# Narrow matrix products widened to all 128 rows in a two-layer decoder

## The reference

```python
x = x + _L0_attn_ref(_layernorm(x), t_k, t_v, t_q, W1, b1, W2, b2)        # scan over the 16 sequences
x = x + _L0_xattn_ref(_layernorm(x), ctx, mask_bf1, Wq, Wk, Wv, Wo, bo, g1, b1, g2, b2)
x = x + _L0_ffn_ref(_layernorm(x), ...)                                    # top 2 of 8 experts
x = x + _L1_attn_ref(_layernorm(x), Wq, Wk, Wv, Wo, bo)                     # ALiBi, 16 heads
x = x + _L1_xattn_ref(_layernorm(x), ctx, ctx, mask_ik0, ...)
x = x + _L1_ffn_ref(_layernorm(x), ...)                                    # top 2 of 8 experts
```

## Time and profile before

| what | value |
|---|---|
| time, median of 3 runs | 746.4 us (741.73 to 748.1) |
| profiled execution, its own time | 753.57 us |
| its span, and mean granted clock | 751.5 us, 0.848 |
| PE busy, share of the span | 603.6 us, 80% |
| DVE, ACT, POOL busy | 483.9, 431.8, 359.0 us |
| rounds of the first rotation | 16, of 6.3 to 14.1 us |
| rounds of the last attention, where steady | 5.24 us |

### The profile page before, as it was taken

One profiled execution on the slowest core, in us unless ns is written; L12 is line 12 of the kernel. 1 busy time (PEld: TensorE's weight loads), 2 busy tenths in 40 slices (PEclk: granted clock), 3 DMA queues, 4 the chain that ended last, 5 costly groups with the idle time before them and its releaser, 6 DMA issues.

```text
span 751.5 us, 18475 instructions
## 1 busy us (share of the span) xinstructions
PE 603.6 (80%) x6145; PEld 484.0 (64%) x6160; DVE 483.9 (64%) x1361; ACT 431.8 (57%) x897; POOL 359.0 (48%) x644
## 2 busy tenths in 40 slices
PE   2797999999999850999937999996997972499970
PEld 1485677777777640999924767664675651499970
DVE  7553545677767543555536999986898976255545
ACT  1452355778667311788814676765686751487840
POOL 5711332445467756466652433421445757365650
PEclk9996555989779565899968999999899996699995
DMA  7749950000000001222163000000000001222215
GB/s 193 231 168 321 330 196 1 2 2 3 1 15 16 22 22 46 72 73 71 52 216 160 2 2 3 1 3 1 2 3 8 28 19 47 53 72 69 68 37 167
DMA packets 41853, 52.59 MB, mean 70 GB/s; under 512 B 11056, under 2 KB 36897, under 8 KB 41473
## 3 DMA queue, kind: packets, MB, share of 16 engines
q1 hardware_dynamic: 37217, 42.07, 18.3%
q0 software_dynamic: 4544, 9.35, 3.8%
HBM read 40.97 MB, written 28.22 MB: 92 GB/s over the span
## 4 chain that ended last, share of the span: by engine, by line
issue 70%; PE 11%; POOL 6%; SPq 2%; DVE 2%; DMA 2%; POOLq 0%; DVEq 0%
PE p_s L1669 5%; POOL yo L1575 5%; PE p_o L1679 3%; PE p_in L1679 2%; DVE x L1626 2%; POOL to_row L1570 1%; SPq L1709 1%; PE p_pT L1661 1%; SPq L286 1%; DMA yo<-context,to_row 1%; DMA context<-xs 0%; DMA back<-yo 0%; SPq L1694 0%; SPq L1698 0%; POOLq L1569 0%
## 5 line engine op out<-in xcount | busy, mean ns | idle before, releaser
L1575 POOL DMA_INDIRECT yo<-context,to_row x78 | 76.1, 976 | 68.0 <-DVE context L1609 36.3
L1633 ACT ACTIVATE context<-pack 128x1156 f32 x78 | 90.6, 1166 | 30.8 <-DVE context L1609 13.4
L1669 PE MATMUL p_s<-xT_f,context 128*128 128x128 f32 x624 | 85.7, 282 | 0.0
L1669 PEld LDWEIGHTS p_s<-xT_f,context 128*128 128x128 f32 x624 | 79.2, 199 | 0.0
L1118 POOL DMA_INDIRECT xs<-send,x_index x64 | 64.1, 1001 | 23.9 <-issue 16.4
L1602 DVE TENSOR_SCALAR context<-p_s,context 128x128 f32<-128x128 f32 x156 | 47.5, 346 | 28.7 <-PE p_s L1669 23.8
L1312 ACT ACTIVATE x_pT<-p_pT 128x512 f32<-128x512 f32 (+1 forms) x96 | 48.8, 526 | 29.6 <-PE p_pT L1415 27.5
L1415 PE MATMUL p_pT<-sq,x_prob 128*128 128x128 f32 x320 | 59.7, 317 | 2.3 <-ACT x_pT L1312 1.6
L1640 ACT ACTIVATE context<-p_s,context 128x128 f32<-128x128 f32 x156 | 47.5, 356 | 21.4 <-PE p_s L1669 12.3
L1154 DVE TENSOR_REDUCE x_top<-p_s 128x12 f32<-128x924 f32 (+2 forms) x48 | 47.0, 1006 | 12.1 <-PE p_s L1401 12.0
L1164 DVE TENSOR_TENSOR x_prob<-p_s,x_top 128x768 f32<-128x768 f32 (+2 forms) x96 | 50.1, 577 | 0.1
(11 more groups left out here) (252 smaller groups left out, 1523.2 us busy)
## 6 DMA issues: line engine op xcount, KB each, us to landing
xs<-in_blank SPq DMA_DIRECT2D x2, 8707.5 KB, 43.3
pack<-in_pack SPq DMA_DIRECT2D x16, 578.0 KB, 8.5
context<-xs SPq DMA_DIRECT2D x78, 64.5 KB
back<-yo SPq DMA_DIRECT2D x16, 256.0 KB, 4.6
yo<-context,to_row POOLq DMA_INDIRECT x78
x<-in_x SPq DMA_DIRECT2D x4, 256.0 KB, 4.5
xs<-send,x_index POOLq DMA_INDIRECT x64
out<-x SPq DMA_DIRECT2D x4, 256.0 KB, 2.3
```

The costliest lines, as they stand in the source:

```text
L1575: nc.gpsimd.indirect_dma_start(yo[:, :], bass.IndirectOffsetOnAxis(to_row[:, n % NY, :], 0), y[:, n % NY, :], None).then_inc(y_stored[n % ...
L1633: nc.scalar.activation(ws[:, n % NW, :], pack[:, bass.ds(e, 1), :].rearrange("p a w -> p (a w)"), ACT.Copy).then_inc(ws_ready, 1)
L1669: ins = mm(p_h[n % 2][k // 2][:, P * (k % 2):P * (k % 2 + 1)], ws[:, n % NW, P * k:P * (k + 1)], xT[:, n % 2, :], start=True, stop=True)
```

## The change

Products that contracted over 1, 3 or 33 rows contract over all 128, and the rows that are added hold zeros in one of the operands:

- the bias products L854 and L1455: the weights were one row of ones and the moving operand the row of the bias; now the weights are the first column of the identity, broadcast along the columns (a one in row 0, zeros below), and the bias is row 0 of a tile of 128 rows with zeros below;
- L865 and L903: the hidden tiles `hT` and `hqT` and the weights `scan_w2T` become 128 rows high, rows 33 to 127 being zeros; POOL clears the two hidden tiles at the start, and the weights come with their zeros from one table in memory, `top_rows`;
- the masks L1389: the mask lies once, in rows 0 (or 0 to 2) of its tile, of which the rest was already cleared; the product takes all 128 rows of it, against a column that is one in these rows and zero elsewhere (the first column of the identity, or column 3 of the triangle `before`). Four transfers place the masks where 16 did.

The order of PE's products is as before. The lines of the changed kernel are from 1 to 5 higher.

```diff
-SCAN_LOADS = 6
+SCAN_LOADS = 5
+        m["first_row"] = m["eye"][:, 0:1].to_broadcast([P, P])
-        m["scan_w2T"] = sb("scan_w2T", [HID + 1, P])
+        m["scan_w2T"] = sb("scan_w2T", [P, P])
-        m["scan_b1r"] = sb("scan_b1r", [1, HID])
+        m["scan_b1r"] = sb("scan_b1r", [P, HID])
@@ start of the rotation on POOL
                 pool.wait_ge(m["loaded_rest"], 16 * m["n_rest"])
-                pool.wait_ge(m["masks_placed"], 64 * NG)
+                for n in ("hT", "hqT"):
+                    nc.gpsimd.memset(m["scan_work"][n], 0.0).then_inc(m["scan_sems"]["set_up"], 1)
+                pool.wait_ge(m["scan_sems"]["set_up"], 2)
+                pool.wait_ge(m["masks_placed"], 64)
@@ loads on SP
-                        load(w2T[0:HID, :], t["scan_w2T"], ls)
-                        load(w2T[HID:HID + 1, :], t["rows"][ROWS.index("s_b2"):ROWS.index("s_b2") + 1, :], ls)
+                        load(w2T[:, :], t["top_rows"][:, P:2 * P], ls)
-                        load(b1r[:, :], t["scan_b1"].rearrange("(a p) -> a p", a=1), ls)
+                        load(b1r[:, :], t["top_rows"][:, 2 * P:], ls)
@@ placing the masks on SP
-                        for g in range(NG):
-                            r0 = STRIP * g
-                            sp.dma_start(m["mask_0"][r0:r0 + 1, :, :].rearrange("a b k -> a (b k)"), mk_0[:, :]).then_inc(m["masks_placed"], 16)
-                            for r in range(3):
-                                sp.dma_start(m["mask_1"][r0 + r:r0 + r + 1, :, :].rearrange("a b k -> a (b k)"),
-                                             mk_1[:, r, :]).then_inc(m["masks_placed"], 16)
+                        sp.dma_start(m["mask_0"][0:1, :, :].rearrange("a b k -> a (b k)"), mk_0[:, :]).then_inc(m["masks_placed"], 16)
+                        for r in range(3):
+                            sp.dma_start(m["mask_1"][r:r + 1, :, :].rearrange("a b k -> a (b k)"), mk_1[:, r, :]).then_inc(m["masks_placed"], 16)
@@ scan, tiles and L854
-        ("hT", [HID + 1, P]), ("hqT", [HID + 1, P]), ...
+        ("hT", [P, P]), ("hqT", [P, P]), ...
-            mm(p_a, ones[0:1, :], b1r[:, :], start=False, stop=True).then_inc(a_ready, 1)
+            mm(p_a, m["first_row"], b1r[:, :], start=False, stop=True).then_inc(a_ready, 1)
@@ attention, masks L1389 and bias L1455
+        rows_on = (m["ident_bf"][:, 0:1] if mask_rows == 1 else m["before"][:, mask_rows:mask_rows + 1]).to_broadcast([P, P])
-                    r = slice(STRIP * strip, STRIP * strip + mask_rows)
-                    mm(to.rearrange("p (h k) -> p h k", k=T), ones_bf[r, :],
-                       m[mask][r, b, :].unsqueeze(1).to_broadcast([mask_rows, len(hs), T]), start=True, stop=False)
+                    mm(to.rearrange("p (h k) -> p h k", k=T), rows_on,
+                       m[mask][:, b, :].unsqueeze(1).to_broadcast([P, len(hs), T]), start=True, stop=False)
-                mm(po_out, m["ones"][0:1, :], m["bo_x0"][0:1, :], start=False, stop=True).then_inc(projected_o, 1)
+                mm(po_out, m["first_row"], m["bo_x0"][:, :], start=False, stop=True).then_inc(projected_o, 1)
```

More of the change, by code:

```diff
@@ L62 @@
 COLS = ["x0_g1", "x0_b1", "x0_g2", "x0_b2", "x1_bq", "x1_bk"]
-ROWS = ["x0_o", "s1_o", "x1_v", "s_b2"]
+ROWS = ["s1_o", "x1_v"]
 def wait(eng, sem, value):
@@ L297, in _ @@
                     nc.gpsimd.memset(tile, 1.0).then_inc(m["scan_sems"]["set_up"], 1)
-                    pool.wait_ge(m["scan_sems"]["set_up"], n + 1)
+                    pool.wait_ge(m["scan_sems"]["set_up"], n + 3)
                 staggered(rotation(FIRST_POOL, {**ts["gpsimd"](pool), **x0["gpsimd"](pool)}))
@@ L467, in _ @@
                         lr = m["loaded_rest"]
-                        rest = [(m[f"bo_{n}"][:, :], t["rows"][ROWS.index(n + "_o"):ROWS.index(n + "_o") + 1, :].to_broadcast([P, P]))
-                                for n in ("x0", "s1")]
+                        rest = [(m["bo_x0"][:, :], t["top_rows"][:, 0:P]),
+                                (m["bo_s1"][:, :], t["rows"][ROWS.index("s1_o"):ROWS.index("s1_o") + 1, :].to_broadcast([P, P]))]
                         rest.append((m["bo_x1"][:, :], t["rows"][ROWS.index("x1_v"):ROWS.index("x1_v") + 1, :].to_broadcast([P, P])))
@@ L704, in scan_work @@
     return {n: own(*shape[1:])[0:shape[0]] for n, shape in (
-        ("hT", [HID + 1, P]), ("hqT", [HID + 1, P]), ("h", [P, HID + 1]), ("a", [P, HID]), ("a2", [P, HID]), ("th", [P, HID]), ("zero", [P, HID]),
+        ("hT", [P, P]), ("hqT", [P, P]), ("h", [P, HID + 1]), ("a", [P, HID]), ("a2", [P, HID]), ("th", [P, HID]), ("zero", [P, HID]),
         ("safe", [P, HID]), ("den", [P, HID]), ("num", [P, 2, HID]), ("slope", [P, HID]), ("eT", [P, P]), ("e", [P, P]), ("da", [P, HID]))}
@@ L787, in b1n @@
             wait(dve, hqT_ready, b)
-            for w_, g_ in ((b1r[:, :], g_b1r), (b1c[:, :], g_b1c)):
+            for w_, g_ in ((b1r[0:1, :], g_b1r), (b1c[:, :], g_b1c)):
                 nc.vector.scalar_tensor_tensor(w_, g_, -GRAD, w_, ALU.mult, ALU.add).then_inc(b1_new, 1)
@@ L794, in w2Tn @@
             wait(dve, out_ready, b)
[L795 removed]
+            nc.vector.scalar_tensor_tensor(w2T[0:HID + 1, :], g_w2T, -GRAD, w2T[0:HID + 1, :], ALU.mult, ALU.add).then_inc(w2T_new, 1)
         def add_out(b, p):
@@ L805, in to_hT @@
             if b == 0:
-                act.wait_ge(set_up, 3)
+                act.wait_ge(set_up, 5)
                 act.wait_ge(m["loaded_scan"], 16 * SCAN_LOADS)
@@ L843, in to_aT @@
             if b == 0:
-                pe.wait_ge(set_up, 3)
+                pe.wait_ge(set_up, 5)
                 pe.wait_ge(m["loaded_scan"], 16 * SCAN_LOADS)
@@ L978, in attention @@
     p_s, p_pT, p_in, p_o = m["p_s"], m["p_pT"], m["p_in"], m["p_o"]
+    if mask:
+        rows_on = (m["ident_bf"][:, 0:1] if mask_rows == 1 else m["before"][:, mask_rows:mask_rows + 1]).to_broadcast([P, P])
     if beside:
@@ L988, in attention @@
         heads = [(0, NH, HG, p_s[:, :, 0:GW].rearrange("p g (h k) -> p g h k", k=T))]
-        banks = [(range(HG * g, HG * (g + 1)), g) for g in range(NG)]
+        banks = [range(HG * g, HG * (g + 1)) for g in range(NG)]
         strips = [[(0, HG, g, 0)] for g in range(NG)]
@@ L1383, in score @@
             if FIRST + b == 0 and mask:
-                pe.wait_ge(m["masks_placed"], 64 * NG)
-            for bank, (hs, strip) in enumerate(banks):
+                pe.wait_ge(m["masks_placed"], 64)
+            for bank, hs in enumerate(banks):
                 to = p_s[:, bank, 0:len(hs) * T]
                 if mask:
-                    r = slice(STRIP * strip, STRIP * strip + mask_rows)
-                    mm(to.rearrange("p (h k) -> p h k", k=T), ones_bf[r, :],
-                       m[mask][r, b, :].unsqueeze(1).to_broadcast([mask_rows, len(hs), T]), start=True, stop=False)
+                    mm(to.rearrange("p (h k) -> p h k", k=T), rows_on,
+                       m[mask][:, b, :].unsqueeze(1).to_broadcast([P, len(hs), T]), start=True, stop=False)
                 else:
@@ L1751 @@
                                          "L1_xattn_bq", "L1_xattn_bk")], axis=1),
-        "rows": np.stack([a[k] for k in ("L0_xattn_bo", "L1_attn_bo", "L1_xattn_bv", "L0_attn_b2")]),
-        "scan_w1T": T(a["L0_attn_W1"]), "scan_w2T": T(a["L0_attn_W2"]), "scan_w2": a["L0_attn_W2"],
+        "top_rows": np.concatenate([np.concatenate([a["L0_xattn_bo"][None], np.zeros((P - 1, P))]),
+                                    np.concatenate([T(a["L0_attn_W2"]), a["L0_attn_b2"][None], np.zeros((P - HID - 1, P))]),
+                                    np.concatenate([a["L0_attn_b1"][None], np.zeros((P - 1, HID))])], axis=1).astype(np.float32),
+        "rows": np.stack([a[k] for k in ("L1_attn_bo", "L1_xattn_bv")]),
+        "scan_w1T": T(a["L0_attn_W1"]), "scan_w2": a["L0_attn_W2"],
         "scan_b1": a["L0_attn_b1"],
```

2 lines of the change are left out of this document (1 added, 1 removed).

## The result

The changed kernel takes **735.22 us** (median of 6 runs, 733.29 to 737.94), the kernel before beside it 747.0 (6 runs): ratio 0.9858, 95% interval 0.9818 to 0.9897, so 1.0 to 1.8% faster. Its profiled execution took 737.5 us, span 735.4, mean granted clock 0.887 (before 753.57, 751.5, 0.848).

The account below looks back on a forecast made before the run. PE was taken to bound the rotation, its clock pricing each round. Clock terms -11.5, -10, -3, rounds +1.6, -2.6, -0.8, start +0.4, last attention +1 sum to -24.9: 728.7 from the profile, 721.5 from the median; forecast 727, range 715 to 744.

Parts of the forecast that it names:

- PE is the bound of the rotation: First rotation: PE busy 78.73 of 79.89 us; a round's price is set by the granted clock, 9.77 us at 1.00.
- The change keeps the clock up: Rotation: wider products hold the clock once up and raise it a round earlier, near 1.00 from about 107 to 240 us.
- Rival 1: Rotation: the clock doesn't care about zero rows, so only product times change; 740 us, chance 0.22.
- The clock terms: Rotation: half-clock time won back, -11.5 us in 154.11 to 234.00, -10 in 95.88 to 134.57, -3 in the tail.
- Rounds with the normalisation: Full-clock rounds from the ninth: only L854's 0.19 saved, masks cost 0.37; +0.18 each, nine rounds, +1.6 us.
- Products: Rotation: products in their neighbours' form save 1.0 us per round at full clock, 0.4 in each of the first two.
- Third and fourth rounds: Rotation, rounds three to seven or so: products -1.0, masks +0.47, about -0.5 us each.
- Start: Before the rotation: two POOL memsets on the path PE waits for, +0.4 us.
- Between the scan and the last attention: Rotation's tail, clock 0.71: up to 11 us from the clock, but POOL sets the pace, so -3 taken.
- Last attention: Serial masks add 0.47 us on PE in 16 rounds, between 0 and 7.5; +1 taken because DVE is full.
- rival 2: Both attentions: serial masks on the score path use up the slack before L1452 and L1154; slower, 759 us, chance 0.09.
- my own sign: Last attention: forecast wrong if its rounds grow from 5.25 us by over 0.2.

Follow-up runs that it names:

- e10: Kernel before with the routing normalisation L1108 moved behind the attention's norm in POOL's order; 748.69 us, ratio 1.005.
- e3: Kernel before plus three zero-weight bf16 products of 128 rows behind the masks in each round of the first rotation; 747.99 us, ratio 1.003.
- e8: Kernel before plus nine zero-weight one-row products, three behind each mask in its strip, per round of the first rotation; median 791.60 us, ratio 1.042.
- e1: Changed kernel with the masks of both attentions back in their row strips, biases and 33-row products still full height; 730.28 us, ratio 0.978.
- e4: Changed kernel with the scan's slope1 put ahead of the routing normalisation L1112 in POOL's order; 734.67 us, ratio 0.985.
- e6: Changed kernel with masks back in row strips and the routing normalisation L1112 moved ahead of slope0 in POOL's order; 712.09 us, ratio 0.962.
- e2: Kernel before with only the masks of both attentions at full height; 748.93 us, ratio 1.001.
- e5: Changed kernel with the routing normalisation L1112 moved ahead of slope0, behind the attention's norm, in POOL's order; 722.16 us, ratio 0.974.
- e12: e6 plus eight zero-weight 128-row products in PE's first rotation wait and three more ahead of L854's counterpart in each of three rounds; ratio 0.970 to kernel before.

## Why the prediction was right, and where its sizes were not

*PE is the bound of the rotation, and its clock the price of a round*: right. e10 shows the bound: work taken out of POOL's chain is worth 0.03 us a round there.

*The change keeps the clock up*: right, and e3 against e8 bears out the cause as I gave it, height passed through, zeros or not (with the strips as the rival left). The rise came at 102.1 and held to 184.0, then from 187.4 to 238.6 (forecast: about 107 to 240). Rival 1 is out. What I had wrong is the share of the masks: I named them first, and e1 shows that the clock rises as well without them; biases or 33 rows alone are enough to do most of it. That the forecast held without the piece named first is in part luck: the change widened all kinds at once. The mean clock of e1's executions (0.879 to 0.892, against 0.885 to 0.898 in the changed kernel) leaves open whether the masks' height adds a little.

*The clock terms*: -10 for 95.88 to 134.57 was near (with its -1.5 of products, 11.5 against 12.5). The term -11.5 + 1.6 for the eighth to fifteenth rounds is **the mis-sized one**: 5.6. Two parts are seen. The round that held the drop of 184.0 to 187.4 took 13.24 instead of 10.1; e4, whose clock stayed up, still took 11.05 in it, so 2.2 of the 3.1 are the clock's. And steady rounds are 10.10, not 9.95, seven times 0.15: about 1.

*Rounds with the normalisation*: -0.19 + 0.37 = +0.18, measured +0.33. The mechanism was right (L854's saving alone counts before L880, the rest becomes idle PE: 0.71 us at L881). Both terms were off a little: e1 against the kernel before gives -0.10 for the products, and changed against e1 +0.43 for the masks. I should also have priced the cure, since I had named the chain: the idle of POOL before L733 was in the same trace.

*Products*: 1.0 us a round at full clock; e10 to e1 gives 0.75 where the normalisation is absent, e10 to e6 0.91 where it is moved. In the first two rounds 0.35 instead of 0.8: in the second of them L881 waits 0.28 us for DVE, where L880 did not wait.

*Third and fourth rounds*, 2.2 us off: I gave them -0.5 each, with the masks at 0.47, though the same text priced them at 0.9 at half clock, where these rounds run. The changed kernel against e1 shows 0.94 in each (10.30 and 10.95 against 9.36 and 10.01). And the products save 0.61 and 0.12 there (9.97 and 10.13 against e1), not 1.0 each.

*Start*: +0.4 for two memsets. e4 starts the scan at 63.3, as forecast; the changed kernel's profiled run at 64.8, with a drop of the clock at 33.8 to 37.2 us that e4's lacks. e2, without the memsets, has that drop too and starts at 64.3; e5, with them, starts at 63.1 without it. So some 1.5 of the 1.9 go with that drop and not with the memsets, whose own share (0.1 to 0.4) is as small as the scatter.

*Between the scan and the last attention*: -3, measured -3.0. The time at half clock between the last round's first product and that mask did fall, from 71.7 to 61.4 us. But PE isn't the bound of the tail (POOL sets the pace), and no run shows that the 3 us come from the clock: the number agrees, its cause isn't shown.

*Last attention*: +1, measured +2.5. Timeline of PE, DVE and ACT in one of its rounds, changed kernel:

```profile
542.12 0.70 PE L1392 MATMUL p_s<-mask,before 128*128 128x308 bf16 x4
542.75 0.80 PE L1404 MATMUL p_s<-x_kT,x_qT 32*128 32x308 f32 x8
543.49 0.33 PE L1370 MATMUL p_in<-sq,x_xn 128*128 128x128 f32 x1
543.62 1.44 DVE L1158 TENSOR_REDUCE x_top<-p_s 128x16 f32<-128x1232 f32 x1
544.01 0.28 ACT L1281 ACTIVATE x_xT<-p_in 128x128 f32<-128x128 f32 x1 [0.99 <-PE p_in L1370]
```

And what PE waited for in four of these rounds of the kernel before (547.6 to 568.6 us: total, times, longest):

```profile
PE p_o L1441 <- DVE x L1180: 1.6, 4, 0.4
PEld p_o L1452 <- DVE x_oT L1174: 1.3, 4, 0.3
```

In the changed kernel both waits are gone, and PE waits for no other engine. L1404 comes 0.49 us later in a round (0.63 behind the mask instead of 0.14), and PE had been busy 19.05 of 21.00, with 0.49 us free; that slack is used up, and rounds are 5.44 to 5.46. I took DVE's slack at L1154 (1.2 us) as the cover. It is gone as well: L1404 ends at 543.55 and DVE's L1158 starts at 543.62. So the condition of rival 2 came true, both slacks were used up, but a round paid 0.2 us and not 0.47, since PE first used up its own waits. ACT waits 0.99 us for L1370, where it waited 0.33, but nobody waits for ACT there, so this decides nothing. By my own sign (rounds over 5.45) this stretch stood right at the edge. The five steady rounds make 1.0 of the 2.5 us; another 1.8 lie in the first four rounds, less 0.3 in the later ones, and why the first four grew isn't followed. The cover that counts is the smallest slack on the ring of waits, not the one that is easiest to see.

The forecast against its own profile, 728.7, was 8.8 too low (737.5): 4.3 from rounds eight to fifteen, 2.2 from three and four, 1.5 each from start and last attention, about 0.5 from the first two, less 1.0 in the fifth to seventh.

## What to carry to other kernels

Where PE is busy and its granted clock is still at half, look at how many rows its products pass, not only at how busy it is. It is no sure cure: the first 40 us of this rotation stayed at half clock in every kernel, but for 6.8 us in e12. Here, giving products of 1 and 33 rows all 128 with zeros made them shorter where they ran alone (the biases, L865 and L903), and cost 0.43 to 0.54 us a round at full clock where they ran side by side in strips (the masks). Take the first, leave the second. And when a product is made shorter, find the wait with the least slack behind it, and move what lies in that chain in the same edit; here that was one entry of a table, worth 1.2% on top of the change and 1.6% on top of e1, against 1.4% for the change itself.

## What was not expected of the hardware

- Adding 0.58 us of one-row products with zero weights to each round made the kernel 4.2% slower (3.0 to 5.4); in the traced execution the clock went to 0.57 with PE busy 75.52 of 76.00 us. 0.82 us of 128-row products cost 0.3% (0.0 to 0.7).
- An fp32 product of one row takes more of PE's time than the same product of 128 rows, if the neighbours have 128: L1455 of the kernel before 0.42 us to the next start, its counterpart L1458 0.22.
- In no kernel did the half clock of the rotation's start end before 100.9 us (the latest, e2, at 112.1), whatever was put into the 40 us ahead of it; the one exception, 6.8 us of full clock in e12, fell back.
